# One fused attention and expert layer: score matmuls of two head pairs in row groups, one more block ahead of the experts, and fewer zeroed rows

## The reference, cut to what matters

```python
xn = _layernorm(x, axis=-1)
x = x + attn(xn, ...) + ffn(xn, ...)

# attn: 16 heads of 16, each token sees the 128 tokens before it
scores = jnp.einsum('bhnqd,bhnkd->bhnqk', qb, kb) * scale
scores = jnp.where(allowed, scores, NEG)
attn = jax.nn.softmax(scores, axis=-1)
out = jnp.einsum('bhnqk,bhnkd->bhnqd', attn, vb)
# a second, latent attention over chunk means: 4 heads of 16
lscores = jnp.einsum('bhsd,bhld->bhsl', rq, rk) * lscale
remote = lat_out @ rout_w + rout_b
gate = jax.nn.sigmoid(local @ gl_w + remote_h @ gr_w)
mixed = gate * local + (1.0 - gate) * remote_h
return mixed @ out_w + out_b

# ffn: each token goes to 8 of 64 experts, chosen by groups
acc + cw[:, None] * ((jax.nn.silu(x @ wg) * (x @ wu)) @ wdn)
```

## Time and profile before

| | us |
|---|---|
| median of 3 runs | 1334.67 |
| lowest and highest run | 1333.65 and 1336.95 |
| the profiled execution | 1338.67 |
| its span, first to last instruction | 1336.9 |
| PE busy | 1255.4 (94%) |
| PE weight loads busy | 1182.4 (88%) |
| DVE busy | 953.3 (71%) |
| ACT busy | 861.7 (64%) |
| POOL busy | 638.7 (48%) |
| mean granted clock of TensorE, in parts of full speed | 0.973 |

### The profile page before, as it was taken

How to read it: one execution, slowest core, us unless ns; L and a number is a source line. 1 busy time by engine, 2 the same in 40 slices (tenths; PEclk the granted TensorE clock), 3 DMA queues, 4 the chain that set the end, 5 groups by cost and what they waited for, 6 DMA issues and landing times.

```text
span 1336.9 us, 38681 instructions
## 1 busy us (share of the span) xinstructions
PE 1255.4 (94%) x9266; PEld 1182.4 (88%) x9267; DVE 953.3 (71%) x4532; ACT 861.7 (64%) x2383; POOL 638.7 (48%) x747
## 2 busy tenths in 40 slices
PE   4957999999999989999999999999999999999996
PEld 3956999999999979999999999999988999999985
DVE  6776666666666637667676676765559898989897
ACT  2323877777777856556565566566657777777774
POOL 7803777777777726565565665656650000000000
PEclk9678999999999979999999999999999999999998
DMA  8107455544333337777777777775545333333330
GB/s 255 63 1 280 163 185 188 206 163 162 123 118 112 114 120 223 211 233 223 224 232 212 233 226 214 233 215 170 175 139 218 107 106 106 106 109 113 116 119 19
DMA packets 152813, 218.40 MB, mean 163 GB/s; under 512 B 24769, under 2 KB 124866, under 8 KB 147650
## 3 DMA queue, kind: packets, MB, share of 16 engines
q1 hardware_dynamic: 80450, 86.77, 20.4%
q0 software_dynamic: 28800, 86.54, 16.9%
q10 hardware_dynamic: 43520, 44.57, 13.1%
HBM read 113.86 MB, written 103.81 MB: 163 GB/s over the span
## 4 chain that ended last, share of the span: by engine, by line
PE 73%; DVE 12%; issue 6%; DMA 3%; ACTq 2%; ACT 2%; DVEq 1%; SPq 1%
PE psS L951 19%; PE psS L824 10%; PE psT L935 5%; PE psO L960 5%; PE psT L838 4%; PE psM L960 4%; DVE x_all L1604 4%; DMA pr<-slot_rows 2%; PE psQ L771 2%; PE psV L811 2%; PE psV L782 2%; PE psQ L792 2%; PE psT L852 2%; PE psT L851 2%; PE psT L850 1%
## 5 line engine op out<-in xcount | busy, mean ns | idle before, releaser
L951 PEld LDWEIGHTS psS<-sm,wt 128*128 128x128 f32 x2560 | 310.8, 193 | 19.5 <-issue 7.8
L951 PE MATMUL psS<-sm,wt 128*128 128x128 f32 x2560 | 316.6, 277 | 1.7 <-ACT sm L1210 0.7
L636 POOL DMA_INDIRECT slot_rows<-x_out_st,idx_st x256 | 257.0, 1004 | 77.5 <-issue 68.6
L1116 ACT ACTIVATE pr<-sm,nmax 128x192 f32<-128x192 f32 x512 | 205.1, 449 | 54.5 <-DVE nmax L1544 52.7
L824 PE MATMUL psS<-kT,qz 128*128 128x192 f32 x1024 | 225.2, 343 | 10.8 <-DVE qz L1487 8.4
L663 POOL DMA_INDIRECT home_rows<-qz,row_idx x160 | 154.6, 966 | 131.0 <-DVE qz L1637 103.4
L663 POOL DMA_INDIRECT home_rows<-sm,row_idx x160 | 155.3, 971 | 86.4 <-issue 45.0
L1228 ACT COPY wt<-shared_mem 128x512 f32 x320 | 183.4, 627 | 4.8 <-issue 4.8
L1216 ACT ACTIVATE prT<-psS 128x256 f32<-128x256 f32 x160 | 61.6, 385 | 187.7 <-issue 100.0
L824 PEld LDWEIGHTS psS<-kT,qz 128*128 128x128 f32 x1024 | 164.3, 192 | 18.4 <-issue 10.3
L1544 DVE CUSTOM_DVE_ANT_0 sm<-psS,pr 128x192 f32<-128x192 f32 x512 | 162.0, 353 | 18.5 <-issue 14.6
(11 more groups left out here) (283 smaller groups left out, 2492.6 us busy)
## 6 DMA issues: line engine op xcount, KB each, us to landing
shared_mem<-home_rows SPq DMA_DIRECT2D x32, 1024.0 KB, 5.1
pr<-slot_rows ACTq DMA_DIRECT2D x120, 272.0 KB
qz<-slot_rows ACTq DMA_DIRECT2D x40, 272.0 KB
slot_rows<-wt SPq DMA_DIRECT2D x32, 272.0 KB
shared_mem<-in_L_ffn_We_gate SPq DMA_DIRECT2D x64, 128.0 KB
shared_mem<-in_L_ffn_We_up SPq DMA_DIRECT2D x64, 128.0 KB
shared_mem<-in_L_ffn_We_down SPq DMA_DIRECT2D x64, 128.0 KB
x_all<-in_L_attn_x SPq DMA_DIRECT2D x4, 1024.0 KB, 9.1
```

What stands on the lines that cost most here:

```text
L636: pool.indirect_dma_start(slot_rows, bass.IndirectOffsetOnAxis(ap=idx_st[:, j, k:k + 1], axis=0), x_out_st[:, j % 2, :], None).then_inc(sc ...
L951: last = mm(psS[:, j % 2, (2 * a + n) * P:(2 * a + n + 1) * P], wt[j % 2][:, a, c, n * F:(n + 1) * F], xsT[:, j % 2, a, c, :], start=(c == ...
L1116: nc.scalar.activation(pr[:, p % 4, par, :], sm[:, p % 4, par, :], ACT.Exp, bias=nmax[:, p % 4, par:par + 1], scale=-1.0).then_inc(probs, 1)
```

## The change

Four things are changed.

1. In the first part (`two` is true where the part starts at block 0) the scores of two neighbouring pairs are issued together at each even step, by `scores_of_two`. Each pair's matmuls use only the 32 partitions that hold its two heads, and so one group of 32 rows of the array; pairs p and p + 1 use different groups and write different banks of `psS`, in turn for each half u of the queries. `qz` then holds two heads instead of eight in a chunk, and is multiplied with `own_half`. PE waits until both earlier pairs are masked, and DVE masks two pairs in a row.
2. In the first part latent scores, maximum, exponential and transposes each come one step sooner; the latent values stay at step 7, ahead of the pair's values.
3. `FIRST` is 18 instead of 17. The adds of expert rows in the last part are dealt out anew: 24 in the resuming block, 16 in each combining one, 24 in the closing one, three a step.
4. Groups of eight tail rows that tokens will fill completely get an index beyond the bound that the indirect DMA is given, and are skipped. DVE computes this with four more operations, POOL prepares one constant for it and two for `own_half`.

```diff
-FIRST = NB // 2 + 1
+FIRST = NB // 2 + 2
...
+            after(nc.gpsimd.tensor_scalar(tail_rows[:], tail_at[:], float(TROWS), float(P), ALU.mult, ALU.add))
...
+            after(nc.gpsimd.tensor_tensor(own_quarter[:], own_head[:, 0:4], own_head[:, 4:8], ALU.add))
+            after(nc.gpsimd.tensor_tensor(own_half[:], own_quarter[:, 0:2], own_quarter[:, 2:4], ALU.add))
...
             for n in range(E // EPD):
                 pool.indirect_dma_start(by_tail, bass.IndirectOffsetOnAxis(ap=tail_idx[:, n:n + 1], axis=0),
-                                        tail_zeros, None).then_inc(tails_cleared, 16)
+                                        tail_zeros, None, bounds_check=(SLOTS + E * P) // TROWS - 1,
+                                            oob_is_err=False).then_inc(tails_cleared, 16)
...
+            def scores_of_two(i, p, nth):
+                n = i * NPAIR + p
+                c = p // PPC
+                if p % PPC == 0:
+                    pe.wait_ge(q_kept, DC * i + c + 1)
+                    pe.wait_ge(k_kept, DC * i + c + 1)
+                if p or nth:
+                    pe.wait_ge(masked, 2 * n)
+                for u in range(2):
+                    for m in (p, p + 1):
+                        r = slice(m % PPC * 2 * HD, (m % PPC + 1) * 2 * HD)
+                        last = mm(psS[:, m % 2, u * WIN:(u + 1) * WIN], qz[r, c, u, 0:2, :].rearrange("p h t -> p (h t)"),
+                                  kT[r, c, u * UQ:u * UQ + WIN], start=True, stop=True)
+                        if u == 1:
+                            last.then_inc(s_ready, 1)
...
-            def body(i, nth, live=True, tail=True, last_tail=True, ahead=True):
+            def body(i, nth, live=True, tail=True, last_tail=True, ahead=True, two=False):
+                early = 1 if two else 0
                 for s in range(NPAIR):
-                    if live:
+                    if live and two and s % 2 == 0:
+                        scores_of_two(i, s, nth)
+                    if live and not two:
                         scores(i, s, nth)
                     if s < 2 and tail:
                         turn_probs(i - 1, s + NPAIR - 2, nth - 1)
                     if s >= 2 and live:
                         turn_probs(i, s - 2, nth)
-                    if s == 7 and live:
+                    if s == 7 and live and early:
+                        latent_values(i)
+                    if s == 7 - early and live:
                         latent_turn(i)
...
-                    if s == 4 and live:
+                    if s == 4 - early and live:
                         latent_scores(i, nth)
...
-                    if s == 7 and live:
+                    if s == 7 and live and not early:
                         latent_values(i)
...
             tail, other = (x for x in (e_a, e_b, e_c) if x is not ends)
             by_dma = lambda x: x.rearrange("p (n e) -> p n e", e=EPD)
+            then(v.scalar_tensor_tensor(tail, n_e, -float(P), psV[:, 0:E], ALU.mult, ALU.add))
+            then(tt(by_dma(tail), by_dma(tail), bcast(tail_rows[:], E // EPD, 1), ALU.subtract))
+            then(ts(tail, tail, float(TROWS - P), SKIPPED, ALU.is_ge, ALU.mult))
             then(v.scalar_tensor_tensor(by_dma(other), by_dma(ends), float(TBLK), bcast(tail_at[:], E // EPD, 1), ALU.mult, ALU.add))
+            then(tt(other, other, tail, ALU.add))
             then(tt(by_dma(tail), by_dma(other), bcast(tail_own[:], E // EPD, 1), ALU.mult))
             then(v.tensor_reduce(other[:, 0:E // EPD], by_dma(tail), AX_X, ALU.add))
...
-            def keep_q(i, c, nth):
+            def keep_q(i, c, nth, two=False):
                 dve.wait_ge(q_staged, DC * i + c + 1)
                 if nth:
                     dve.wait_ge(s_ready, NPAIR * (i - 1) + PPC * (c + 1))
-                v.tensor_tensor(qz[:, c, :, :, :], bcast(qT[:, c, :].rearrange("p (u t) -> p u t", u=2), HPC, 2),
-                                bcast(bcast(own_head[:], UQ, 2), 2, 1), ALU.mult).then_inc(q_kept, 1)
+                n, own = (2, own_half) if two else (HPC, own_head)
+                v.tensor_tensor(qz[:, c, :, 0:n, :], bcast(qT[:, c, :].rearrange("p (u t) -> p u t", u=2), n, 2),
+                                bcast(bcast(own[:], UQ, 2), 2, 1), ALU.mult).then_inc(q_kept, 1)
...
-                    if live:
+                    if live and two and s % 2 == 0:
                         mask_pair(i, s, nth)
-                    if closing and s in (1, 2, 5, 7):
-                        n = (1, 2, 5, 7).index(s)
-                        if n == 0:
-                            dve.wait_ge(acc_done, NB - 1)
-                        combine(NB - 2 + n // 2, 2 + n // 2, range(n % 2 * 4, n % 2 * 4 + 4))
+                        mask_pair(i, s + 1, nth)
+                    if live and not two:
+                        mask_pair(i, s, nth)
+                    if closing:
+                        for n in range(3 * s, 3 * s + 3):
+                            if n == K:
+                                dve.wait_ge(acc_done, NB - 1)
+                            combine(NB - 3 + n // K, (NB - 3 + n // K) % ROWS, (n % K,))
                     if resuming and s >= NPAIR // 2:
-                        for n in range(2):
-                            add_row(i, 4 * s - 2 * NPAIR + n)
+                        for n in range(3):
+                            add_first_row(6 * s - 3 * NPAIR + n)
                     if combining:
                         add_row(i, 2 * s)
                     if s == 0 and tail and last_tail:
...
             def add_row(i, n):
-                combine(2 * (i - FIRST) + n // K, 2 * ((i + 1) % 2) + n // K, (n % K,))
+                combine(2 * (i - FIRST) + 1 + n // K, 2 * ((i + n // K) % 2) + 1 - n // K, (n % K,))
+
+            def add_first_row(n):
+                combine(n // K, n // K, (n % K,))
```

53 lines of the change are left out of this document (31 added, 22 removed).

## The result

The changed kernel took 1320.23 us, median of 4 runs (1319.14 to 1321.38), beside 1334.16 us for the kernel before (1333.12 to 1336.95): a ratio of 0.989, interval 0.987 to 0.991. The forecast was 1312 us, range 1303 to 1343; the result lies inside that range and 2 us above the 1304 to 1318 us to which the prediction gave its main chance. The profiled execution took 1319.14 us, its span is 1317.4.

The account below looks back on a forecast made before the run. PE was taken as full in the first part, PE and DVE in the last. 1338.7 us, with attention's end moved from 475.0 to 466.4 and -14.5 behind, gave 1315.6; less 4.0 for the median, 1312 us, range 1303 to 1343.

Parts of the forecast that it names:

- The overlap: First-part scores: two row groups stream together, weight loads limit; a set takes 0.95 us, 3.8 instead of 5.7 a block.
- The rival in which the groups take turns: First-part scores: row groups overlap at every other border or not at all; s = -0.1, 1342 us; chance 0.17.
- The switch: First-part scores: changing between 128-row and 32-row matmuls, eight times a block, costs 0; upper bound 1.3 us a block.
- The end of attention: First part: attention's end moves from 475.0 by one 21.0 us block, less 0.8 and 18 s, to 466.4 us.
- who waits instead: First-part blocks: PE waits for ACT's copies in odd steps; net cost 0.3 us a block, bounds 0 and 1.2.
- The scatters: POOL, first part: skipped zeros let scatters start 10 us earlier, about 120 us, and end near 460 us.
- One block fewer: Last part: saves 21.7 us, less 4.1 for adds in the resuming block and 3.1 in the closing: -14.5 us.
- From execution to median: Whole kernel: 4.0 us subtracted from 1315.6, since the profiled execution before lay that far above its median: 1312 us.
- Switching drains the array: Rival, first-part scores: overlap works but switching costs 1.3 us a block; s = 0.3, 1335 us, no change; chance 0.12.
- overlap is better than weight loading allows: Rival, first part: attention ends before 461, scatters hold the part, 1306 us; lower part of the forecast, no chance of its own.
- POOL's scatters stay the end: Rival, first part: tail DMAs don't shorten, experts start at 475, only the last part gains: 1320 us; chance 0.08.
- ACT becomes the limit: Rival, first-part odd steps: ACT's long steps 3 and 7 cost 1.2 instead of 0.3; s = 0.8, 1326 us; chance 0.08.

Follow-up runs that it names:

- the maximum first: The changed kernel with DVE's latent maximum ahead of the mixing sums in the first part: 1314.06 us, ratio 0.985; again on a chip with pauses 1568.31 us, ratio 1.003.

## Why the prediction held, and where its steps didn't

The main mechanism was right: the two row groups run side by side, the block shrinks, and the end of attention moves by it. The number came out close partly by luck, since two terms of the block's sum were wrong by the same amount in opposite directions.

**The overlap.** The forecast stood on the choice that two row groups stream at the same time, and they do. It took weight loads as the next limit and put a set at 0.95 us. They aren't the limit: the four pairs of matmuls of a set start 0.163 us apart, as single ones did before, so the streaming of a set takes 4 x 0.163 = 0.65 us, 2.6 us a block where the sum had 3.8. Weight loads of the two groups start together as well (last section). The rival in which the groups take turns is out: it needed 1.3 us a set.

**The switch.** The prediction took 0 for each change between 128-row and 32-row matmuls, with an upper bound of 0.163 us, 1.3 us a block. The runs show nearly all of that bound. Median distances in us between the starts of matmuls, from 150 to 440 us:

| | before | changed |
|---|---|---|
| last score matmul to first transpose | 0.162 | 0.251 |
| first to second transpose | 0.109 | 0.165 |
| projection of queries and keys to first score matmul | 0.112 | 0.205 |
| behind that projection, first score matmul to the second (changed: to the second pair) | 0.165 | 0.267 |

So leaving the 32-row form costs 0.09 + 0.06 = 0.15 us. Entering costs 0.09 + 0.10 us behind the projection, the same behind the latent scores, and 0.12 behind values, whose sets started late before as well. With four sets a block, the fourth behind the turn of the mixed rows and taken like the first two, that is about 1.3 us. The weight loads show what is lost; first the changed kernel at such a change, then the kernel before at the same place:

```profile
311.96 0.63 PEld L847 LDWEIGHTS psS<-kT,qz 32*128 32x128 f32 x8 [0.33 <-issue]
312.81 0.31 PEld L862 LDWEIGHTS psT<-ident,pr 128*128 128x128 f32 x3 [0.22 <-issue]
```

```profile
312.42 0.73 PEld L824 LDWEIGHTS psS<-kT,qz 128*128 128x128 f32 x4
313.12 0.41 PEld L838 LDWEIGHTS psT<-ident,pr 128*128 128x128 f32 x3
```

Before, the load for the first transpose starts at 313.12 us, with the last score matmul; in the changed kernel it starts 0.25 us behind that matmul, after an idle 0.22. The Trainium skill, TensorEngine Tiling, Key Properties, says that changing the tiling mode drains TensorE. The trace agrees, with 0.12 to 0.2 us at each change. The scores with both changes fell from 5.7 to 4.0 us a block, by 1.7 instead of 1.9: 1.2 us gained on the overlap and 1.3 lost on the switch, against the sum. That they cancel is luck.

**Waits.** Taken as 0.3 us a block, and about that came: 1.7 less the measured 1.4. The bigger items are the odd steps, in which PE waits for ACT's copies, and against them 0.24 us less for latent values and the mixed turn. So s is 1.4 us, where the forecast had 1.6.

**The end of attention.** Predicted 466.4, measured 471.1. Blocks 0.2 us longer make 3.4. The other big part is one that the sum didn't hold: the last block lost 5.4 us by a wait and the clock behind it. Against these, this execution's start ran some us sooner, which varies from run to run (PE's first score matmul 112.4 instead of 114.8 us, and latent scores began at 114.9 to 122.4 us in kernels of nearly the same start). The step "who waits instead" looked at ACT's copies in odd steps and never asked behind which work the moved latent_max stands: mix_sums, on DVE, in the same step.

**The scatters.** The prediction expected 120 to 460 us, and 121.8 to 456 was measured, but half of its reason for the start was wrong. Halving the zeros was to take 10 us; it took 3.9, because the DMA engines didn't share evenly what was left (above). The rest of the shift came because the whole start stage ran sooner: with all rows zeroed the first scatter stands at 124.8 us, against 130.5 before.

**One block fewer.** Predicted -21.7 + 4.1 + 3.1. The resuming block took 27.26 us instead of 21.37, so 5.9. That isn't all the adds. Here is the distance from its latent scores to the next, as a stretch (columns of the earlier trace rows): before; with 17 blocks; with 17 blocks and the maximum first, all three with 16 adds; and the changed kernel, with 24.

```profile
1006.90:1028.30 21.40, 19.41 (x150) 18.60 (x149) 20.16 (x77) 15.76 (x52) 0.00 (x0) 1.00 0.56 202
988.90:1011.90 23.00, 21.01 (x149) 19.80 (x149) 20.16 (x75) 15.92 (x51) 0.00 (x0) 0.93 0.52 189
987.70:1012.10 24.40, 22.42 (x149) 21.20 (x149) 20.17 (x75) 15.86 (x51) 0.00 (x0) 0.86 0.49 177
1000.80:1028.00 27.20, 23.53 (x149) 21.88 (x149) 23.70 (x83) 15.70 (x51) 0.00 (x0) 0.81 0.57 203
```

DVE's work is the same in the first three, and the block grows by just what PE's does, 1.6 and 3.0 us, with the clock at 0.50 for none, 3.4 and 6.8 us of it. In the changed kernel the clock is down from 1010.5 to 1020.7 us, and PE has no idle time from 1016 on. DVE then waits for it; the releaser isn't named in the row, but the wait ends with the score matmuls that PE started at 1022.18 us:

```profile
1023.13 0.35 DVE L1581 CUSTOM_DVE_ANT_0 sm<-psS,pr 128x192 f32<-128x192 f32 x1 [2.06 <-issue]
```

Kernels with 24 adds whose clock is down for 6.8 us take 26.7 to 26.8 us here, those with 16 adds and 6.8 us take 24.2 and 24.4. So an estimate from these rows is 2.4 us for the eight adds instead of 4.1, and the rest of the 5.9 for the clock. Why it falls there in every later kernel that was traced and not in the kernel before isn't shown; PE has one wait of 1.6 us in that block before as well, and two of 1.5 in the changed kernel. The closing cost 1.7 instead of 3.1: the adds moved into the first step lie in DVE's idle time ahead of the projection's add, and more of the later ones lay beside other waits.

**From execution to median.** By the profiled executions the forecast was 1315.6 and the result 1319.1, a miss of 3.5: +4.7 for the end of attention, +1.8 for the resuming block and +0.6 for the other last blocks, less 1.4 for the closing and 2.2 for the experts. The other 5 us are the last step: 4.0 were subtracted because before's profiled execution lay above its median, and the changed one's lay 1.1 below. That a profiled run's offset would carry over was an assumption with no row behind it.

**Rivals.** "Switching drains the array" was right in its cost of 1.3 us and wrong in the sum, and "overlap is better than weight loading allows" was right in its overlap; the result lies between them because both hold. "POOL's scatters stay the end" gave 1320 by another route and isn't what happened; it does describe both kernels with 17 blocks. "ACT becomes the limit" was near in kind, with DVE's order as the cause behind ACT; its own sum is off by 0.1, since 5.7 - 3.8 - 1.2 is 0.7 and gives 1328 us. Likewise eight loads of 0.11 are 0.88 and not 0.90 us, which changes nothing.

The best kernel of the study is the changed one with the maximum first: 1314.06 us, 0.985.

## What to carry to other kernels

Matmuls of two independent pairs that need only 32 rows each stream in half the time in two row groups. Each change of form costs 0.12 to 0.2 us, so issue several at once: with four sets a block the changes ate 1.3 of the 2.6 us that the overlap gave. When steps are moved sooner on one engine, look on every other engine at what they now stand behind, and above all in the last turn of the loop, where the work that hid the wait is missing. On a PE that is 98% busy a wait's price isn't its length: 0.5 to 2 us of idleness can cost 2 to 5 us through the clock, so closing small gaps may be worth more than removing work. When half of a DMA's groups are skipped, expect half of the time only if every DMA engine loses its half. A resource that ends a few us behind the one that you shorten (here the scatters) needs its own remedy or other work as a filler.

## What the runs showed of the hardware

**Two row groups start together.** The recorded starts in us of the eight score matmuls in the set at 311.96 us, and of the set at 573.76 with the groups in turn (digits ahead of the point left out where they repeat):

```
alternating: 311.965 .972   312.232 .238   .394 .401   .557 .564
in turn:     573.761 .775   574.028 .041   .190 .204   .353 .366
```

Pairs start 7 ns apart when the groups alternate and 14 ns when they don't. The Trainium skill, TensorE: Matmul & The Clock Gate, Part 3, gives up to 4 ns for neighbours in different row groups; these f32 pairs show 7. The weight loads of such a pair stand as close, at 311.963 and 311.970 us. The records don't name the group, so which matmuls form a pair in the second order isn't shown.

**The clock after short gaps.** The granted clock fell to 0.50, its lower level of 1.2 GHz, behind an idle 1.82 us in the changed kernel, and behind single waits of 0.52 us in the kernel with late latent steps, in blocks that otherwise kept PE full; behind equal waits in most of its blocks it didn't. In these places it came back after 3.4 to 10.2 us.

**Chips on which everything pauses.** On two of the chips the kernel before took 17 and 19% longer. Stretches of the kernel with the maximum first there: one while the scatters run, then most of the scatters' time, then the two blocks behind them.

```profile
300.00:302.00 2.00, 0.32 (x2) 0.35 (x3) 1.93 (x12) 0.94 (x4) 0.24 (x2) 0.65 0.19 70
...
200.00:500.00 300.00, 248.73 (x1640) 214.48 (x1638) 122.43 (x666) 173.20 (x563) 178.37 (x202) 0.84 0.36 124
553.00:592.00 39.00, 38.83 (x315) 34.45 (x315) 23.34 (x127) 32.10 (x107) 0.00 (x0) 1.00 0.00 1
```

Just ahead of 301.7 us PE stood still for 2.3 us, ACT for 2.6 and POOL for 1.8, and the clock falls behind it. Between 200 and 500 us there are 20 moments of over 0.2 us in which PE, DVE, ACT and POOL all stand still, 1.3 us the longest; the same kernel on the other chip has none between 200 and 440 us. Most blocks take 27 to 30 us under the scatters and 19.2 to 19.5 right behind them; the scatters themselves need (547.4 - 122.7) / 255 = 1.67 us each instead of 1.31. The experts' part, in which POOL sends the results home, is longer too: 641 us from the first load to the first latent scores behind it, instead of 532. The last part, where POOL issues nothing, is 21.7 us a block as everywhere. So the pauses go with POOL's DMAs. What they are no view shows, and no run took the DMAs away to prove it.
